# Attention maxima taken four strips at a time

## The reference, cut to what matters

```python
qh = _split_heads(q @ wq + bq, B)        # q: layer-normed x
kh = _split_heads(k @ wk + bk, B)        # k, v: the context, 154 tokens
vh = _split_heads(v @ wv + bv, B)
scores = jnp.einsum('bhqd,bhkd->bhqk', qh, kh) * scale
probs = jax.nn.softmax(scores, axis=-1)
out = jnp.einsum('bhqk,bhkd->bhqd', probs, vh)
return out @ wo + bo
```

## Time and profile before

| | us |
|---|---|
| median of 3 timed runs | 1383.21 |
| lowest and highest of them | 1383.08, 1385.77 |
| profiled execution, whole | 1370.34 |
| profiled execution, span | 1368.6 |
| TensorE busy in the span | 1205.5 (88%) |
| VectorE busy | 702.4 (51%) |
| ScalarE busy | 448.4 (33%) |
| GpSimd busy | 292.8 (21%) |
| mean granted TensorE clock | 0.924 |

### The profile page before, as it was taken

The page is one execution under the profiler, slowest core; times in us unless marked ns, Lnnn a source line. Parts: engine busy times, 40 slices in busy tenths (PEclk is TensorE's granted clock), DMA queues, the critical chain, the costliest instruction groups (busy, mean ns, idle before and its releaser), DMA issues.

```text
span 1368.6 us, 19327 instructions
## 1 busy us (share of the span) xinstructions
PE 1205.5 (88%) x6360; PEld 761.6 (56%) x6361; DVE 702.4 (51%) x1997; ACT 448.4 (33%) x842; POOL 292.8 (21%) x347
## 2 busy tenths in 40 slices
PE   6999999999879999999988669999667699999993
PEld 4534434434434454445334559999556545888862
DVE  7273474478876545654552521111276752455557
ACT  3322222233445354544434113333243201333320
POOL 2111111130030011010100041111123563255560
PEclk9999999999988999999888579999877789999997
DMA  9999999200000000001000845555309322555538
GB/s 301 338 336 327 334 333 333 81 14 1 0 1 1 1 1 1 1 1 34 1 0 1 270 161 194 171 182 186 114 29 349 115 89 92 144 162 166 168 111 314
DMA packets 140489, 186.75 MB, mean 136 GB/s; under 512 B 8737, under 2 KB 124961, under 8 KB 140289
## 3 DMA queue, kind: packets, MB, share of 16 engines
q1 hardware_dynamic: 130864, 159.28, 37.5%
q0 software_dynamic: 9552, 26.52, 5.3%
HBM read 83.71 MB, written 102.06 MB: 136 GB/s over the span
## 4 chain that ended last, share of the span: by engine, by line
PE 74%; DVE 13%; ACT 4%; issue 3%; DMA 3%; POOL 2%; SPq 0%; POOLq 0%; DVEq 0%; ACTq 0%
PE psum L2005 13%; PE psum L1266 6%; PE psum L1277 6%; PE psum L1055 6%; PE psum L2217 5%; PE psum L1074 3%; PE psum L936 3%; PE psum L2274 3%; PE psum L1995 2%; PE psum L2251 2%; PE psum L2298 2%; PE psum L2195 2%; PE psum L2034 2%; DVE arena L2836 2%; PE psum L947 2%
## 5 line engine op out<-in xcount | busy, mean ns | idle before, releaser
L2005 PE MATMUL psum<-arena 128*128 128x512 f32 x432 | 199.6, 604 | 0.0
L2836 DVE TENSOR_REDUCE arena<-psum 128x4 f32<-128x616 f32 x128 | 101.5, 796 | 98.6 <-PE psum L2217 97.3
L2005 PEld LDWEIGHTS psum<-arena 128*128 128x128 f32 x432 | 77.7, 190 | 102.8 <-issue 102.0
L2217 PE MATMUL psum<-arena 32*128 32x308 f32 x512 | 104.0, 498 | 16.9 <-DVE arena L2836 16.0
L1182 POOL DMA_INDIRECT ys<-xnT,arena x96 | 92.1, 959 | 90.9 <-DVE xnT L1159 68.4
L2418 ACT ACTIVATE arena<-psum,arena 128x512 f32<-128x512 f32 x72 | 49.0, 685 | 160.4 <-PE psum L2005 150.7
L1894 POOL TENSOR_TENSOR x_tok<-x_tok,add_row 128x1024 f32<-128x1024 f32 x16 | 38.3, 2400 | 266.6 <-ACT xn L1759 266.5
L2509 ACT ACTIVATE arena<-psum 128x2048 f32<-128x2048 f32 x40 | 75.0, 1874 | 60.1 <-PE psum L2255 41.6
L1266 PEld LDWEIGHTS psum<-side,arena 128*128 128x128 f32 x736 | 87.8, 196 | 2.7 <-ACT side L1311 1.6
L1055 PE MATMUL psum<-arena,xn 128*128 x384 | 87.1, 380 | 2.4 <-ACT xn L1105 1.9
L1266 PE MATMUL psum<-side,arena 128*128 128x128 f32 x736 | 88.2, 279 | 1.0 <-ACT side L1311 1.0
(11 more groups left out here) (418 smaller groups left out, 2090.4 us busy)
## 6 DMA issues: line engine op xcount, KB each, us to landing
xs<-zeros SPq DMA_DIRECT2D x8, 8576.0 KB, 60.0
arena<-in_W SPq DMA_DIRECT2D x31, 1024.0 KB, 5.0
xn<-xs SPq DMA_DIRECT2D x64, 134.0 KB, 2.4
arena<-in_gate_up SPq DMA_DIRECT2D x4, 2048.0 KB, 15.9
arena<-xs SPq DMA_DIRECT2D x32, 134.0 KB, 2.3
arena<-in_down SPq DMA_DIRECT2D x4, 1024.0 KB, 14.6
arena<-ys SPq DMA_DIRECT2D x4, 1024.0 KB, 12.5
arena<-ys SPq DMA_DIRECT2D x2, 2048.0 KB, 14.0
```

Of the source, the lines that this page charges most:

```text
L2005: ins = pe.matmul(bank[dict(hn=4, r=5, z=6, xn=7)[k]][:], lhs[:, cols], r, start=(start and n == 0), stop=(stop and n == len(w) - 1))
L2217: ins = pe.matmul(bank[most_bank(n, k) + i][:, 0:2 * M].rearrange("p (h m) -> p h m", h=2), qhT[rows, n % 3, c, t * P:(t + 1) * P], keys[r ...
L2836: dve.tensor_reduce(neg[:, n % 2, t, 2 * pair:2 * pair + 2, 2 * c:2 * c + 2], psum[:, most_bank(n, k):most_bank(n, k) + 2, 0:2 * M].rearra ...
```

## The change

Of the sixteen places of a slot eight keep a pair. The other eight become four steps `four`, each of which does the work of two pairs at once: all four strips go at the same time, into the weighing's banks 0 to 3, and VectorE takes the maxima of the four banks with one reduction. The step `four(r)` stands between weighing r and the next: it waits for the exponential of weighing r, and the next weighing waits for its maxima (for r = 3 that is weighing 4 of the next slot). A pair now waits for the pair before it and no longer for a step of four in between. After a step of four `advance` does six pieces, and `advance_early` does six in place of four after every maximum where it is not for slot 0. The maxima of slot 0, taken ahead of the slots, stay in pairs.

```diff
             yield from behind("project", n - 1, 0)
             yield from most()
+            yield from four(0)
             yield from behind("project", n - 1, 1)
-            yield from most()
             yield from itertools.islice(second, 1)
             yield ("weigh", n, 1)
-            yield from most()
             yield ("rests", n, 0)
             yield ("values", n, 0)
-            yield from most()
+            yield from four(1)
             yield ("values", n, 1)
-            yield from most()
...
             yield from ahead("turn", n + 2, 0)
-            yield from most()
+            yield from four(2)
             yield ("untangle", n, 1)
             yield from ahead("turn", n + 2, 1)
-            yield from most()
             yield from token("normalise", 3, tri)
             yield from itertools.islice(second, 1)
             yield ("weigh", n, 3)
-            yield from most()
             yield from ahead("query", n + 2, 0)
-            yield from most()
+            yield from four(3)
             yield from token("tri_turn", tri, 0)
...
+            def four(n, k, _, r):
+                l, b = n // G, n % G // GB
+                t, c = k // 4, k // 2 % 2
+                pe.wait_ge(weighed, weighed_at[n - 1, r] + 1)
+                for j in range(4):
+                    rows = slice(32 * j, 32 * j + 32)
+                    ins = pe.matmul(bank[j][:, 0:2 * M].rearrange("p (h m) -> p h m", h=2),
+                                    qhT[rows, n % 3, c, t * P:(t + 1) * P], keys[rows, l, c, b, :, 0:M],
+                                    start=True, stop=True, tile_position=(32 * j, 0))
+                ins.then_inc(most_done, 2)
...
                 if weighed_at[n, r]:
                     pe.wait_ge(weighed, weighed_at[n, r])
+                    if r != 4 and (n, (4, 0, 1, 2)[r]) in fours:
+                        pe.wait_ge(most_found, fours[n, (4, 0, 1, 2)[r]])
+                    elif r == 4 and (n - 1, 3) in fours:
+                        pe.wait_ge(most_found, fours[n - 1, 3])
...
+            def four(n, k, last, _):
+                t, c = k // 4, k // 2 % 2
+                dve.wait_ge(most_done, 16 * n + last + 1)
+                dve.tensor_reduce(neg[:, n % 2, t, 0:4, 2 * c:2 * c + 2],
+                                  psum[:, 0:4, 0:2 * M].rearrange("p b (h m) -> p b h m", h=2),
+                                  AX.X, ALU.max, negate=True).then_inc(most_found, 2)
...
-                    if op[0] == "most" or op[1] == SLOTS - 1:
-                        advance()
-                    if op[0] == "most":
+                    if op[0] in ("most", "four") or op[1] == SLOTS - 1:
+                        advance(6 if op[0] == "four" else 4)
+                    if op[0] in ("most", "four"):
                         advance_early(op[1])
```

More of the change, by code:

```diff
@@ L397, in most, with four @@
                 return [("most", n + 1, next(count))] if n + 1 < SLOTS else []
+            def four(r):
+                return [("four", n + 1, next(count), next(count), r)] if n + 1 < SLOTS else []
             def behind(*op):
@@ L481, in most_bank @@
             return 0 if n == 0 and k % 2 else 4
+        pairs = [op for op in flow() if op[0] == "most"]
+        pair_ahead = {op: pairs[i - 1] for i, op in enumerate(pairs) if i}
+        fours = {(op[1] - 1, op[4]): 16 * op[1] + op[3] + 1 for op in flow() if op[0] == "four"}
         weighed_at = {(n, r): 5 * n + k for n in range(SLOTS) for k, r in enumerate((4, 0, 1, 2, 3))}
@@ L2206, in most @@
                 elif n:
-                    pe.wait_ge(most_found, 16 * n + k)
+                    _, m, i = pair_ahead["most", n, k]
+                    pe.wait_ge(most_found, 16 * m + i + 1)
                 if k == 0:
@@ L2345, in mha_tensor @@
                 elif op[0] not in ("tanh", "settle", "normalise", "norm1", "norm2"):
-                    dict(late_turn=late_turn, late_product=late_product, first=first, second=second, turn=turn, query=query, most=most, shift=shift, weigh=weigh, rests=rests, values=values,
+                    dict(late_turn=late_turn, late_product=late_product, first=first, second=second, turn=turn, query=query, most=most, four=four, shift=shift, weigh=weigh, rests=rests, values=values,
                          untangle=untangle, back=back, project=project, tri_turn=tri_turn, tri=tri)[op[0]](*op[1:])
@@ L2541, in mha_scalar @@
                     normalise_scalar(act, int(op[0][4]), op[1])
-                elif op[0] not in ("most", "untangle", "project", "tri", "settle", "rests", "finish", "product", "late_product"):
+                elif op[0] not in ("most", "untangle", "project", "tri", "settle", "rests", "finish", "product", "late_product", "four"):
                     dict(late_turn=late_turn, first=first, second=second, turn=turn, query=query, shift=shift, weigh=weigh, values=values, back=back, tri_turn=tri_turn,
@@ L2816, in advance_early @@
             def advance_early(n):
-                pieces = 8 if n == 0 else 4
+                pieces = 8 if n == 0 else 6
                 while early and pieces > 0:
@@ L2890, in finish, with advance @@
                     pass
-            def advance():
-                pieces = 4
+            def advance(pieces):
                 for s in (4, 3, 5):
@@ L2901, in mha_vector @@
             for op in flow():
-                if op[0] in ("most", "untangle", "project", "tri", "settle", "late_product"):
+                if op[0] in ("most", "four", "untangle", "project", "tri", "settle", "late_product"):
                     if op[0] == "project" and op[2] == 1:
                         finish(3 + 2 * (op[1] // G))
-                    dict(most=most, untangle=untangle, project=project, tri=tri, settle=settle,
+                    dict(most=most, four=four, untangle=untangle, project=project, tri=tri, settle=settle,
                          late_product=late_product)[op[0]](*op[1:])
-                    if op[0] == "most" or op[1] == SLOTS - 1:
-                        advance()
-                    if op[0] == "most":
+                    if op[0] in ("most", "four") or op[1] == SLOTS - 1:
+                        advance(6 if op[0] == "four" else 4)
+                    if op[0] in ("most", "four"):
                         advance_early(op[1])
```

## The result

The changed kernel takes 1398.49 us (median of 10 runs, 1392.84 to 1404.48) against 1384.03 us for the kernel before beside it (10 runs, 1380.79 to 1392.18). The ratio is 1.0095 with a 95% interval of 1.0069 to 1.0122: slower by about 1%, or 13 us (the medians alone differ by 14.5). On the 1383.2 us of the prediction the ratio gives 1396.3, which lies inside its range of 1375 to 1398; the median as it stands, 1398.49, is half a microsecond outside.

What follows compares the result with a forecast made beforehand. TensorE's own queue, busy 93 to 94% of slots 2 to 5, was taken as the bound. Full-clock walk -1.95 plus clock +7.65 gave +5.7 us on 1383.2, so 1388.9 us; range 1375 to 1398.

Steps and rivals of the forecast that it cites:

- the waits: All seven slots walked at full clock to their second rests, TensorE's saving set against new waits: -1.95 us in sum.
- the clock: 4.5 new stretches of TensorE's lower clock in slots 2 to 4, at 1.7 us each: +7.65 us.
- The prices: A step of four costs TensorE one pair's price, 0.8 us for its matmuls; VectorE's reduction of 1232 elements takes 1.43 us.
- The walk through slot 4: Slot 4 step by step at full clock: 2.9 us saved, 6.1 us waited against 1.7, so 1.5 us longer.
- Slot 5: Without a second normalising, its second rests were to start at 668.7 in place of 670.46: -1.75 us.
- The walk through slots 0 and 1: Full-clock walk to the second rests, context products covering waits: -2.5 us in slot 0, -0.4 in slot 1.
- the saving comes through: Rival: VectorE's pieces and the exponentials end in time, half of TensorE's 20.2 us stays, 1373 us; chance 0.20.
- The long chain: Rival: four(3) waits for the exponential behind the second normalising, slots 1 to 4 +2.5 each, clock +5: 1398 us; chance 0.13.
- The reductions: Rival: VectorE's longer reductions become the bound, 17.6 of 20.2 us vanish, 1380.6 us; chance 0.20 together with waits without clock.

Runs made afterwards that it cites:

- the fastest kernel: The changed kernel with four(0) and four(1) taken back into pairs and four(3) moved behind the second rests: 1355.20 us, 0.9876 of the kernel before.

## Why the prediction was right or wrong

**The sign, and the size.** Slower was forecast with 0.55, and by 5.7 us; it is 13, more than twice as much, at the upper end of the range. In the profiles the slots grew by 13.5 us, 7.8 more than forecast: by the estimate above the waits are 10.9 us over (+8.9 against -1.95) and the clock 3.1 us under (+4.6 against +7.65). That the sum came nearer than its larger term is luck. The steps:

**The prices were right.** The matmuls of a step of four take 0.80 us, the reduction 1.437 us (1.43 predicted).

**The walk through slot 4 was right in the main.** Predicted against measured waits: weighing 1 0.46 and 0.56, rests 1.06 and 0.59, weighing 2 0.65 and 0.74, four(2) 0.6 and 0.58, weighing 3 0.4 and 0.70, four(3) 3.2 and 2.36, the query 0 and 0.53 (the predicted ones, with 0.3 at a pair, add up to 6.7 us, not to the 6.1 that the prediction names). The second rests came 34.29 us (slot 3) and 33.95 us (slot 4) after the slot's start; 34.25 was predicted. Slot 5 came out at -1.73 against -1.75, but that is in part luck: TensorE's idle time grew there by 3.0 us, 0.5 more than its work shrank, while the clock up to the second rests was 1.00 in place of 0.95.

**The walk through slots 0 and 1 was wrong, by 10.4 us in sum, about half of it waits and half clock.** The step "slot 0 has no normalising before its last exponential and no projection to evict, and context products stand behind three of its fours" counted the products as cover. The third of them needs the ring bank of untangle 1, and VectorE does the untangling behind four(2)'s reduction and six pieces, in slot 0 whole-tile steps of the quantisation. The trace shows the stops, 2.57 and 2.40 us. The idle time of both slots grew by 7.2 us against 2.9 in the walk (5.8 us saved, the slots 2.9 us shorter), and the clock took 5.6 us more, where the prediction took "as many as today". With the pieces at 4, and without four(2), slot 0 was 4.3 and 5.6 us shorter. In slot 1 the second of these brought 1.0 us only.

**The clock was wrong in place and too large in size.** 7.65 us were set against slots 2 to 4, most of it slots 3 and 4. Those two kept the full clock in the profiled execution with the same stops of 2.36 us; slot 2 lost 4.9 us behind its second rests alone, and slots 0 and 1 fell to 0.81 and 0.94 (0.91 and 0.97 before). Slot 5 even gained 4.6 us, from 0.88 to 1.00. The prediction's rule that frequent short stops lower the clock does not tell these slots apart: between the first and the second rests slots 2, 3 and 4 have the same stops (0.73 or 0.74, 0.31, 0.58, 0.70, 0.53 and 2.36 us), and only slot 2 lost its clock behind them. Profiles of close relatives have it in other slots. Across the kernels the median clock and the time go together: 0.937 at 1355 us, 0.933 at 1362, 0.927 at 1375, 0.920 at 1384. If time at the lower level costs half of itself, the fastest kernel could owe all of its gain to it: (1 - 0.937) x 1355 = 85 us against (1 - 0.922) x 1373 = 107 us, for 17.7 us of difference. Whether the clock is the cause or follows from fewer stops, these numbers do not say. It is not so throughout: with four(3) taken out the clock is that of the kernel before and the time is 11 us longer.

**What I did not see is which of the steps carries the loss.** The prediction put its weight on four(3). That stop is real, but the runs put the loss on four(0): without it 0.9956, it alone 1.0086. The traces show by what way. With four(0) in the order the norm on VectorE ends later, and with it come later the second normalising, the exponential behind it and the second rests. From the start of slot 4 the second normalising starts after 27.3 to 28.2 us in all eight kernels that have a four(0) (27.41 in the changed one) and after 25.1 to 26.1 us in the five others of the experiments; the second rests start after 33.4 to 34.7 us and after 31.1 to 32.7. Taking out four(2) or four(3) leaves the normalising of slot 3 where it is (27.75 and 27.76 against 27.75), taking out four(0) moves it to 26.13. The kernel before has it at 25.75. The prediction had this later end in its walk (27.45 us in slot 4), but charged it to four(3), which only waits for it. What in four(0) delays the norm is not parted: the longer reduction, or the six pieces in place of the eight that stand behind two pairs. With four pieces everywhere the norm ended later still (27.83 us in slot 4), which speaks for the pieces; held back behind the projection's eviction they changed little (27.26).

Up to the first rests of slot 4 the kernel before has TensorE busy for 12.79 of 12.79 us and VectorE for 9.17, so every wait that a longer reduction brings there is added to the slot:

```profile
594.15:606.94 12.79, 12.79 (x121) 7.39 (x121) 9.17 (x21) 6.23 (x6) 0.00 (x0) 1.00 0.00 1
```

Between the first and the second rests TensorE already stopped for 1.7 us of 20, and there a step of four pays. That four(0)'s early place did not help, and that the norm ended late there too, speaks for VectorE's load in this part and not for the place among its neighbours. This is argued, not shown; a kernel that takes load off VectorE there was not tried.

The rival "the saving comes through" holds for the kernels with the steps of four in the later half of the slot. "The long chain" came nearest in numbers: +10 us of waits and +5 us of clock against +8.9 and +4.6, with +8.6 of the waits in its slots 1 to 4. Its place, the exponential behind the second normalising, is where slots 2 to 4 wait; in slot 1 it is the context product. It had a chance of 0.13. The reductions did not become the bound: VectorE is busy for 48 to 63% of slots 2 to 6. What they cost is waits.

**Open:** why slots 3 and 4 kept their clock where slot 2 did not, how much of each ratio is clock and how much waits, since only one execution of each kernel was profiled, and how the changed kernel itself would compare on the chips of the experiments.

## What to carry to other kernels

A saving on the busiest engine is worth its size only where the next engine in the chain has slack in that very stretch: read busy time by stretches of 10 us, not by the average, before a step is made larger. When a producer's banks are shared with another chain, list for each new step what it waits for, what waits for it, and who reuses the ring bank that is evicted behind it on the same queue. Follow a longer step on a side engine to the end of its queue's work: here 0.64 us more of reduction in one place, and fewer norm pieces behind it, went with a later end of the norm, and with it of the whole second half of the slot. Stops of half a microsecond to two cost more than themselves where TensorE's clock falls behind them; a gauge stretch of unchanged work shows how much.

## What the runs showed of the hardware

Four fp32 matmuls of 308 columns on four row strips (eight records) took 0.80 us at full clock, the same as two on two strips (0.79, four records). VectorE's maximum over 1232 elements from four banks took 1.44 us against 0.80 for 616. With one step of four a slot, four(0), TensorE stopped in slot 4 for 0.56, 0.59, 0.32, 0.61 and 1.06 us, and in slots 2 to 4 unchanged work behind the last of these stops took 3 to 5 us more, at granted clocks of 0.86 to 0.93 over the slot where the kernel before had 0.96 to 1.00. The same stops do not always bring this: with 2.36 us ahead of four(3) slot 2 lost 4.9 us and slots 3 and 4 nothing. The same program gave 1354.65 and 1363.39 us in two executions, with mean clocks of 0.937 and 0.929.
